# Flamingo gated block: GpSimd makes the scores' operand ahead of the third context chunk instead of behind it

## What is computed

```python
q = layernorm(x) @ Wq.T + bq; k = context @ Wk.T + bk; v = context @ Wv.T + bv     # 16 heads of 8
attn = softmax(einsum('bhtd,bhcd->bhtc', q, k) / sqrt(8))
x = x + tanh(g_xattn[0]) * (einsum('bhtc,bhcd->bhtd', attn, v) @ Wo.T + bo)
probs = sigmoid(layernorm(x) @ router_w.T + expert_bias); top_w, top_idx = top_k(probs, 8)
x = x + tanh(g_ffn[0]) * (routed experts, weighted by top_w + one shared expert)
```

## Time and profile before

| | |
|---|---|
| median of 3 runs | 1141.21 us (1140.9 to 1142.85) |
| the profiled execution: time, span | 1140.58 us, 1139.1 us |
| busy PE, DVE, ACT, POOL | 1069.6, 969.8, 845.1, 610.7 us |
| chain that ended last, by engine | PE 45%, POOL 21%, issue 16%, DVE 9% |
| `q_st` (line 603) and `q_blk` (line 585) in that chain | 3% and 3% |

### The profile page before, as it was taken

How to read it: one execution, slowest core, us unless ns; L and a number is a source line. 1 busy time by engine, 2 the same in 40 slices (tenths; PEclk the granted TensorE clock), 3 DMA queues, 4 the chain that set the end, 5 groups by cost and what they waited for, 6 DMA issues and landing times.

```text
span 1139.1 us, 37969 instructions
## 1 busy us (share of the span) xinstructions
PE 1069.6 (94%) x12090; PEld 708.6 (62%) x12090; DVE 969.8 (85%) x1706; ACT 845.1 (74%) x1812; POOL 610.7 (54%) x1042
## 2 busy tenths in 40 slices
PE   2798899999999999999999999879999999999998
PEld 1366677777777777777777777644555555555554
DVE  3677788888888888888888888669999999999998
ACT  2566577777777777767777776658888888888886
POOL 4887888888888888888888988000000000000000
PEclk9799999999999999999999999889999999999999
DMA  6786866757667767568577552146777767776673
GB/s 129 162 179 150 187 155 171 170 137 182 154 143 184 156 161 176 135 159 180 139 182 164 132 144 61 25 138 209 231 226 232 239 227 226 234 236 226 225 240 115
DMA packets 201816, 197.06 MB, mean 173 GB/s; under 512 B 161999, under 2 KB 168207, under 8 KB 201782
## 3 DMA queue, kind: packets, MB, share of 16 engines
q1 hardware_dynamic: 188292, 174.14, 58.2%
q0 software_dynamic: 11520, 20.99, 6.5%
q10 hardware_dynamic: 1970, 1.49, 0.7%
HBM read 109.96 MB, written 12.55 MB: 108 GB/s over the span
## 4 chain that ended last, share of the span: by engine, by line
PE 45%; POOL 21%; issue 16%; DVE 9%; SPq 3%; DMA 2%; POOLq 2%; ACT 1%; DVEq 0%; ACTq 0%
PE bank L1368 15%; PE bank L1340 15%; PE bank L1170 4%; PE bank L1184 4%; DVE part_max L897 3%; POOL ctx_parts L495 3%; PE bank L1203 3%; POOL q_st L603 3%; POOL q_blk L585 3%; POOL w_in L468 3%; POOL w_in L470 2%; POOL w_out L516 2%; POOL w_out L515 2%; DVE rec L1024 2%; PE bank L1239 2%
## 5 line engine op out<-in xcount | busy, mean ns | idle before, releaser
L701 ACT ACTIVATE p_exp<-bank 125x448 f32<-125x448 f32 x768 | 400.2, 544 | 193.4 <-PE bank L1184 192.4
L897 DVE TENSOR_REDUCE part_max<-bank 128x1 f32<-128x500 f32 x672 | 420.9, 672 | 71.6 <-PE bank L1203 71.2
L1184 PE MATMUL bank<-q_st,k_stk 97*125 97x224 f16 x1536 | 275.6, 264 | 15.5 <-DMA q_st<-neg_row 8.9
L1203 PE MATMUL bank<-kparts,q_blk 128*128 128x500 f16 x672 | 256.3, 385 | 13.4 <-DVE part_max L897 11.2
L1184 PEld LDWEIGHTS bank<-q_st,k_stk 97*125 97x125 f16 x1536 | 197.2, 139 | 80.3 <-ACT p_exp L701 16.4
L1368 PE MATMUL bank<-ctT,w_ring 128*128 128x448 f16 x960 | 234.0, 353 | 3.0 <-DVE ctT L1072 3.0
L778 ACT ACTIVATE ctT<-bank 128x448 f32<-128x448 f32 x320 | 173.6, 543 | 40.6 <-PE bank L1340 16.1
L1072 DVE TENSOR_TENSOR ctT<-k_stk,ctT 128x448 f16<-128x448 f32 x320 | 198.2, 619 | 0.5 <-ACT ctT L784 0.4
L1170 PE MATMUL bank<-p_exp,v_sb 125*25 125x168 f32 (+1 forms) x6144 | 187.9, 263 | 0.4 <-ACT p_exp L701 0.4
L784 ACT ACTIVATE ctT<-k_stk 128x448 f16<-128x448 f32 x320 | 181.7, 568 | 5.5 <-DVE k_stk L1066 3.2
L1340 PE MATMUL bank<-q_hi,w_ring 128*128 128x448 f16 x640 | 174.0, 354 | 2.4 <-ACT k_stk L767 2.4
(11 more groups left out here) (157 smaller groups left out, 1241.1 us busy)
## 6 DMA issues: line engine op xcount, KB each, us to landing
v_sb<-c_scratch SPq DMA_DIRECT2D x114, 448.0 KB, 4.0
k_stk<-kparts SPq DMA_DIRECT2D x384, 93.8 KB, 3.5
ctx_in<-in_ctx_dram SPq DMA_DIRECT2D x30, 672.0 KB
k_stk<-c_scratch SPq DMA_DIRECT2D x38, 448.0 KB, 3.9
w_scratch<-w_out POOLq DMA_DIRECT2D x80, 128.0 KB, 3.2
w_in<-in_L_ffn_w_gate_dram POOLq DMA_DIRECT2D x160, 32.0 KB, 3.3
w_in<-in_L_ffn_w_down_dram POOLq DMA_DIRECT2D x80, 64.0 KB, 3.4
ctx_in<-in_ctx_dram SPq DMA_DIRECT2D x30, 78.0 KB
```

The lines of the kernel that those rows point to most:

```text
L701: act.activation(p_exp[0:KP, j % PR, f * 448:(f + 1) * 448], ST[f][0:KP, 0:448], ACT.Exp).then_inc(exp_done, 1)
L897: v.reduce_max(part_max[:, i // NCH, i % NCH:i % NCH + 1], SM[i % NSM][:, 0:CK], axis=AX.X).then_inc(sm_maxed, 1)
L1184: last = pe.matmul(ST[f][0:KP, (g % 2) * GC:(g % 2 + 1) * GC], k_stk[0:97, u, g, j * KP:(j + 1) * KP], q_st[0:97, u, g, :, :].rearrange("p ...
L1203: pe.matmul(SM[i % NSM][:, 0:CK], rows, kparts[:, u, 0, c * CK:(c + 1) * CK], start=True, stop=True).then_inc(sm_done, 1)
```

## The change

In GpSimd's body the block that makes `q_st`, with its waits, becomes a function `scores_operand`, which is called in the loop over the chunks ahead of the third one, in place of behind the loop. Nothing else changes, on no other engine.

```diff
+            def scores_operand(step):
+
+                if isinstance(step[0], int) and num(step) == 1:
+                    first_rows()
+                if on(step, 1):
+                    h, u = back(step, 1)
+                    b = num((h, u))
+                    until(pool, st_done, (b - 1) * (2 * KT))
+                    for g in range(HG):
+                        last = pool.tensor_tensor(q_st[0:96, u, g, :, :],
+                                                  q_stk[0:96, g, bass.ds(b * T, T)].unsqueeze(1).to_broadcast([96, HG, T]),
+                                                  stack_mask[:, :].unsqueeze(2).to_broadcast([96, HG, T]), ALU.mult)
+                    last.then_inc(qst_made, 1)
+
             def body(step):
...
                 for c in range(NCH):
+                    if c == NCH - 1:
+                        scores_operand(step)
                     if on(step, -1):
                         split_ctx(back(step, -1), c)
                     if on(step, 2):
                         expert_pairs(back(step, 2), PREP[step[1]][c:c + 1])
-                if isinstance(step[0], int) and num(step) == 1:
-                    first_rows()
-                if on(step, 1):
-                    h, u = back(step, 1)
-                    b = num((h, u))
-                    until(pool, st_done, (b - 1) * (2 * KT))
-                    for g in range(HG):
-                        last = pool.tensor_tensor(q_st[0:96, u, g, :, :],
-                                                  q_stk[0:96, g, bass.ds(b * T, T)].unsqueeze(1).to_broadcast([96, HG, T]),
-                                                  stack_mask[:, :].unsqueeze(2).to_broadcast([96, HG, T]), ALU.mult)
-                    last.then_inc(qst_made, 1)
```

## The result

The changed kernel took 1144.05 us (median of 12 runs, 1141.25 to 1148.39), the kernel before beside it 1141.42 us (12 runs, 1138.23 to 1145.25). The ratio is 1.0022 with a 95% interval of 1.0012 to 1.0033, so the change costs 2.5 us (1.4 to 3.8). The forecast was +1.7, in a range of 1140.3 to 1145.0. The profiled execution of the changed kernel took 1144.12 us, its span is 1142.6 us; before it was 1139.1 us.

What follows compares the result with a forecast made beforehand. GpSimd's unwaiting list, with TensorE at almost equal pace, bounds the attention phase. TensorE stands +3.5 us at batch 20, +1.4 at batch 30, +1.7 at step 32's tokens through GpSimd's late start: 1142.9 us, range 1140.3 to 1145.0.

Steps and rivals of the forecast that it cites:

- Step 1: GpSimd's `q_st`: ready 1.8 us earlier in odd steps, 6.4 in even; `st_done` wait covered by 10 us, no cost.
- Step 2: Third split and transpose 2.10 us later: no TensorE cost; SP's row binds in even batches, 1.4 us behind GpSimd's odd step.
- Step 3: Row DMA right behind a transpose on SP's queue: taken as 2.5 us to the scores, between 2.05 and 3.15.
- rival B: Row behind the transpose lands late, every even batch starts on it: +2.1 us at 3.02, +3.0 at about 4; chance 0.16.
- A round of GpSimd keeps its 41.27 us: GpSimd's loop: no instruction is added or removed, so two steps still take 41.27 us.
- rival C: GpSimd's loop-end register work and branch no longer hidden: up to 8 us less 1 slack; sign, round over 41.35; chance 0.05.
- Step 4: Program start: SP's third transpose of step 2 comes 1.9 us later, GpSimd carries 1.9 onward; bounds 0 and 2.1.
- The sum at batch 20: Behind GpSimd's pause in step 21: scores at 488.8 against 485.77, +3.1 us, from start delay, transpose and landing.
- The recovery of 0.45 behind a wait: TensorE's tile sequence, disturbed by a wait at batch 20, loses 0.45 us more, making +3.5.
- Batch 29: TensorE behind GpSimd's third pause: some 0.6 us of loss (0.1 waiting and 0.45) falls away.
- A: Start delay does not pass through, 0 in place of 1.9: result -0.5 us, or -0.9 with quick landing; chance 0.17.
- D: SP's 19.0 us of waits on `q_st` go, TensorE is free after pauses: some 3.4 us gained; chance 0.08.

Runs made afterwards that it cites:

- run 11: The changed kernel measured once more, for a second trace: 1144.89 us, ratio 1.0034 to the kernel before.
- run 2: The kernel before with `q_st` ahead of the third chunk in steps 1 to 3 only: 1140.85 us, ratio 1.0009.
- run 1, e1: The changed kernel with `q_st` behind the third chunk in steps 1 to 3, as before: 1142.38 us, ratio 1.0029.
- run 6: The changed kernel with SP issuing the row DMA ahead of the third transpose from step 4 on: 1145.99 us, ratio 1.0061.
- run 7, e8: The changed kernel with row DMA ahead of the third transpose, reciprocal in PSUM, `q_st` as before in steps 1 to 3: 1141.44 us, ratio 1.0014.
- run 4: The changed kernel with the reciprocal written in place in PSUM and read there by `o_nrm`: 1140.65 us, ratio 1.0009.
- e6, run 5: The kernel before with the reciprocal left in PSUM and read there by `o_nrm`: 1140.47 us, ratio 1.0008.
- e10, run 8: The kernel before with SP issuing the row DMA ahead of the third transpose from step 4 on: 1140.02 us, ratio 1.0009.
- e14: The kernel before measured once more under its own label, for a second trace: 1140.18 us, ratio 1.0002.
- run 10: The changed kernel without the loads of the expert pairs behind the first five: 1136.95 us, ratio 0.9963.
- run 9: The kernel before without the loads of the expert pairs behind the first five: 1148.40 us, ratio 1.0082.
- run 3: The changed kernel, but in step 30 `q_st` is made behind the third chunk and pair, as before: 1141.51 us, ratio 1.0018.

## Why the forecast was right, and where not

The size and the sign hold: +1.7 was forecast, +2.5 [1.4, 3.8] measured, and +3.9 [2.5, 5.4] in run 11. It is a little more than the 0.2% that the forecast put between "same" and "slower". The agreement in size is mostly luck: the forecast's +1.7 is a late start that GpSimd carries to the tokens, while the start alone gave +1.0 with zero in its interval (run 2), and the change without it kept the whole loss (run 1). Two more terms were off in opposite directions, and the largest one was missing.

**The bound.** Right. GpSimd waits for nobody behind step 4 in either kernel; TensorE sits on the row DMA at batches 4, 10 and 20 and nowhere else with a wait of note. Runs 6 and 7 show it from the other side: a TensorE that stands 3.6 and 4.4 us closer to GpSimd's step 31 waits 3.7 and 4.4 us for the tokens. The last term of the sum, the tokens of step 32 as the bound of the phase, was right as a mechanism. In the changed kernel it did not come to bear: TensorE began the tokens at 695.82 without a wait.

**Step 1** (`q_st` earlier, no new wait): right for the loop, no wait on `st_done` appears. In step 1 of the program the moved block brings its wait for the first stacked queries ahead of the third split, and there GpSimd waits longer. The kernel before, then the changed one:

```profile
POOL q_st L603 <- DMA q_stk<-q_lo: 3.3, 1, 3.3
```

```profile
POOL q_st L589 <- DMA q_stk<-q_lo: 5.1, 1, 5.1
```

**Step 2** (third split and transpose later): right. Rows of even batches go out 483.60 - 482.16 = 1.44 us behind the end of the odd step, 1.4 was forecast; binding moves from odd to even batches.

**Step 3** (landing behind a transpose, taken as 2.5 of 2.05 to 3.15): missed. It is 1.96 us from row to scores, even a little under what a row with nothing ahead of it took, 508.09 - 506.04 = 2.05. One transpose ahead on the queue adds nothing that these traces show. In the Trainium skill (DMA: Bandwidth & Descriptors, Two DMAs through the same engine are not ordered) descriptors of one queue of a DMA engine start in order and then overlap. I had read a delay into it from the 3.02 us of the program's first row, which no even batch repeats. The rule itself is not contradicted by 1.96. The late landing of rival B is out; but its "every even batch" came true with the quick landing.

**"A round of GpSimd keeps its 41.27 us"**: missed, and this is the step that the loop's part of the loss comes from, with 1.0 to 1.4 us between steps 4 and 31. The round is 41.36 to 41.41 in most of the changed kernel's rounds, so it lies over TensorE's 41.35, and every even batch from 4 to 20 starts on its row. It is the sign that was named for rival C, with 1.0 to 1.4 us in place of up to 8, but not its cause: the loop's register work does not show, since `q_blk` at 438.32 follows the subtraction of 437.20 + 1.16 = 438.36 without a gap. What shows is a hundredth of a us in many operations: the groups of GpSimd's instructions from 290 to 455 us (times, then busy us and mean ns), before and then changed:

```profile
L603 POOL TENSOR_TENSOR q_st<-q_stk,stack_mask 96x224 f16<-96x224 f16 x32 | 16.8, 556 | 0.1
...
L585 POOL TENSOR_TENSOR q_blk<-q_hi,head_mask 128x896 f16<-128x896 f16 x8 | 13.4, 1673 | 0.0
```

```profile
L589 POOL TENSOR_TENSOR q_st<-q_stk,stack_mask 96x224 f16<-96x224 f16 x32 | 16.9, 563 | 0.1
...
L599 POOL TENSOR_TENSOR q_blk<-q_hi,head_mask 128x896 f16<-128x896 f16 x8 | 13.5, 1691 | 0.1
```

Run 4 took a part of it away with `o_nrm`, but not in these two, which stay at 562 and 1689 ns there. What makes them longer is not shown.

**Step 4** (the start, 1.9 us through SP): seen and not resolved. From `q_blk` of step 3 to that of step 4 it is 23.4 to 23.95 us in six traces with `q_st` ahead there and 21.4 to 23.3 in six with it behind (before, e1, e6, e8, e10, e14), 1.2 us more in the mean. Counted from the first `q_blk`, step 4 comes 80.4 to 81.8 us behind it in the first six and 78.6 to 80.6 in the others, 1.6 us more in the mean: 1.8 more from `q_blk` of step 1 to that of step 2, where the longer wait above lies, 1.5 less from step 2 to 3, and the 1.2. The absolute time of step 4 is the same in the mean, 106.1 and 105.95, because the first `q_blk` of a program falls anywhere between 24.1 and 27.4 us. Run 2 has the delay alone, +1.0 [-0.5, +2.5]; run 1 takes it away and gains nothing. So the delay is there with about 1.6 us within the program, on another road than the forecast's; how much of it reaches the time, between 0 and 1.6, stays open.

**The sum at batch 20**, without the start: counted from `q_blk` of step 4 the scores of batch 20 came 1.2 us later than before (381.02 against 379.80), and 3.1 - 1.9 = 1.2 was forecast. Two errors cancel there: the landing is 0.54 shorter, GpSimd's list 0.55 longer.

**The recovery of 0.45 behind a wait**: missed, by the clock. Behind the wait of 2.28 the next step took 1.6 us more than 21.08. So batches 21 and 22 together took 42.96 us, where the forecast has 41.8 and the kernel before 42.88: the 1.5 us gained there were lost again to a clock of 1.2 GHz.

**Batch 29**: forecast -0.6, measured +3.3, and +1.6 in the second trace, where the clock did not fall. The term that is missing from the sum is `o_nrm` in step 30. I had put moved work only against waits and queues, and not against what the other engines do at that moment. In the Trainium skill (GPSIMD Engine Reference, Key points) GpSimd shares its SBUF interfaces with VectorE, which matters for VectorE instructions "with two SBUF inputs". The traces agree on the condition, 2.22, 2.16, 2.06 and 1.77 us with two inputs in SBUF against 0.39 with one of them in PSUM, and show the size: in these four `o_nrm` ended 0.26 us behind the end of the last of the four `q_st`, so at most 0.13 us of its 0.39 can lie ahead of that end. It need not be the last one: in step 31 of the kernel before it was the third of four, and in run 10 the cast behind them. What decides it is not shown.

Of the rivals, A (no delay) fits the absolute time of step 4 and, within their intervals, runs 1 and 2, but not the steps counted within the program, and its -0.5 missed the round, the clock and step 30. D (the 19.0 us of SP's waits turn into a gain) is out: they went to zero and time went up.

**What stays open.** Why a wait of 2.01 at batch 20 lowers the clock (run 4), and one of 2.19 does not, at batch 10 of the changed kernel or at batch 20 of run 7; and behind which of GpSimd's operations a held `o_nrm` comes through. What makes GpSimd pause for 2.3 us at three of its weight loads; without the loads the pauses are absent. And no version here that does the whole work beats the kernel before: runs 2, 4, 5 and 8 lie within their intervals of it, the others are slower.

## What to carry to other kernels

If one engine works through its list without a wait and its pace is the pace of the phase, then look first at what a new order of that list does to that pace: waits that vanish from another queue's view, like SP's 19.0 us here, were worth nothing by themselves. Before moving a run of operations on GpSimd, look up in VectorE's timeline which operations with two inputs in SBUF will stand beside it, since one of them in the wrong place can be held for the whole run; reading one input from PSUM removed this here. Where two engines have almost the same pace, a tenth of a microsecond in a round decides which of them is waited for, so it has to be measured and not assumed.

## What the runs showed of the hardware

- A VectorE `tensor_tensor` of 128x224 f32 with both inputs in SBUF took 0.39 us alone, 1.16 beside one GpSimd subtraction of 1.15 (run 6; `o_nrm` at 283.58, GpSimd at 283.35), and 1.77 to 2.22 beside four GpSimd multiplications back to back. It is not slowed in proportion, it is held: in all these it ended 0.24 to 0.26 us behind the end of a GpSimd operation, mostly the last of the run, but the third of four in the kernel before (0.84 us) and the cast behind the four in run 10 (3.11 us). GpSimd's next operation then took 0.16 us longer in step 30 of the changed kernel (the cast, 0.77 in place of 0.62) and in step 31 of the kernel before (the fourth `q_st`, 0.71 in place of 0.55). With one input in PSUM `o_nrm` took 0.39 in the same place.
- Less work on GpSimd made the kernel 9.3 us slower in the old order (run 9), where it brought this meeting into every round, and 4.2 us faster in the new one (run 10).
- A row DMA issued right behind a DMA transpose on the same queue was in use 1.96 us after its issue, as quickly as one with nothing ahead.
- TensorE's granted clock fell to 1.2 GHz behind waits of 2.0 to 2.3 us at batch 20 in five traces (the change twice, runs 1, 3 and 4), and behind 2.28 and 2.33 at batch 4 (runs 1 and 3), and it then cost 1.5 to 1.7 us more on top of the wait; behind 2.04 to 2.19 at batch 10 (the change twice, run 4), 2.19 at batch 20 of run 7, and behind 1.08 and 1.74 at batch 21 of the old order, it did not.
